# Layer 2's bias: from two TensorE products to a VectorE addition out of PSUM

## The reference, cut to what matters

```
W   = adj * adj                            # nodes x nodes
out = einsum('bnf,nm->bmf', x, W) + bias   # bias: 512 values, one for each feature
x   = layernorm(x + out, axis=-1)          # (x - mean) / sqrt(var + 1e-5)
```

## Time and profile before

| | us |
|---|---|
| median of three runs | 2135.47 |
| the profiled execution, its own time | 2135.43 |
| its span in the trace | 2133.6 |
| TensorE products, busy | 2043.6 (96%) |
| VectorE, busy | 1609.4 (75%) |
| ScalarE, busy | 1061.7 (50%) |
| GpSimd, busy | 131.9 (6%) |

### The profile page before, as it was taken

One profiled execution on the slowest core, in us unless ns is written; L12 is line 12 of the kernel. 1 busy time (PEld: TensorE's weight loads), 2 busy tenths in 40 slices (PEclk: granted clock), 3 DMA queues, 4 the chain that ended last, 5 costly groups with the idle time before them and its releaser, 6 DMA issues.

```text
span 2133.6 us, 34670 instructions
## 1 busy us (share of the span) xinstructions
PE 2043.6 (96%) x13500; PEld 1840.6 (86%) x13500; DVE 1609.4 (75%) x4339; ACT 1061.7 (50%) x1965; POOL 131.9 (6%) x198
## 2 busy tenths in 40 slices
PE   7899999999999999999999999999999999999997
PEld 6788888988888888888988888898888888888896
DVE  6477868778687787878777786877868787787875
ACT  5445536455453645546454553645545364453643
POOL 0000000000000000000100000000000000000000
PEclk9999999999999999999999999999999999999998
DMA  4100000000000000000000000000000000000000
GB/s 139 50 11 11 21 21 11 21 21 21 11 21 21 11 21 11 21 20 11 31 11 20 11 21 21 11 21 21 21 11 21 21 11 20 11 21 20 11 11 20
DMA packets 23652, 44.70 MB, mean 21 GB/s; under 512 B 2624, under 2 KB 2880, under 8 KB 23488
## 3 DMA queue, kind: packets, MB, share of 16 engines
q1 hardware_dynamic: 23488, 42.48, 5.7%
HBM read 25.70 MB, written 16.78 MB: 20 GB/s over the span
## 4 chain that ended last, share of the span: by engine, by line
PE 90%; ACT 4%; DVE 4%; issue 2%; DMA 0%; SPq 0%; POOL 0%; POOLq 0%; ACTq 0%; DVEq 0%
PE psum L494 11%; PE psum L479 11%; PE psum L332 10%; PE psum L419 6%; PE psum L340 6%; PE psum L468 6%; PE psum L519 5%; PE psum L525 5%; PE psum L520 5%; PE psum L469 5%; PE psum L336 5%; PE psum L423 3%; PE psum L506 3%; PE psum L575 2%; ACT xs L693 1%
## 5 line engine op out<-in xcount | busy, mean ns | idle before, releaser
L966 DVE TENSOR_TENSOR zs<-psum,zs 128x512 fp32r<-128x512 f32 (+1 forms) x456 | 262.9, 609 | 191.9 <-ACT zs L693 191.8
L693 ACT ACTIVATE zs<-psum 128x512 fp32r<-128x512 f32 (+1 forms) x456 | 235.8, 535 | 196.7 <-PE psum L479 164.5
L494 PE MATMUL psum<-xs,zs 128*128 128x256 f32 x2048 | 270.8, 285 | 0.0
L494 PEld LDWEIGHTS psum<-xs,zs 128*128 128x128 f32 x2048 | 258.1, 191 | 5.0
L693 ACT ACTIVATE full<-psum 128x512 f32<-128x512 f32 x160 | 94.8, 593 | 284.1 <-PE psum L494 146.5
L340 PE MATMUL psum<-ident,full 128*128 128x128 f32 x1220 | 172.3, 274 | 11.8 <-DMA full<-in_L_gnn_wk_dram 5.1
L419 PE MATMUL psum<-vs,zs 128*128 128x512 f32 x512 | 141.2, 397 | 26.0 <-ACT vs L693 26.0
L340 PEld LDWEIGHTS psum<-ident,full 128*128 128x128 f32 x1220 | 140.0, 141 | 28.5 <-issue 8.2
L693 ACT ACTIVATE vs<-psum 128x512 fp32r<-128x512 f32 x128 | 76.6, 598 | 131.7 <-PE psum L525 131.7
L332 PE MATMUL psum<-vs,zs 128*128 128x512 f32 x512 | 140.2, 396 | 0.7 <-ACT zs L693 0.7
L419 PEld LDWEIGHTS psum<-vs,zs 128*128 128x128 f32 x512 | 91.7, 188 | 54.2 <-DVE full L1225 36.1
(11 more groups left out here) (198 smaller groups left out, 5153.6 us busy)
## 6 DMA issues: line engine op xcount, KB each, us to landing
full<-in_x_dram SPq DMA_DIRECT2D x32, 512.0 KB, 3.5
out_dram<-full SPq DMA_DIRECT2D x32, 512.0 KB, 2.7
full<-in_L_gnn_W_lang_dram SPq DMA_DIRECT2D x2, 1024.0 KB, 5.4
full<-in_L_gnn_W_grav_dram SPq DMA_DIRECT2D x2, 1024.0 KB, 8.1
full<-in_L_gnn_W_O_dram SPq DMA_DIRECT2D x2, 1024.0 KB, 5.4
full<-in_L_gnn_W_V_dram SPq DMA_DIRECT2D x2, 1024.0 KB, 5.0
full<-in_adj_dram SPq DMA_DIRECT2D x1, 256.0 KB, 2.6
full<-in_L_gnn_bias_dram SPq DMA_DIRECT2D x1, 256.0 KB, 6.9
```

The source lines that it names most:

```text
L494: last = mm(halves(bank)[:, n, :], y[:, e, n * P:(n + 1) * P], HTH[s][:, e, :], start=(y is ZH[s][kind] and e == 0 and n == 0), stop=(y is ...
L693: return nc.scalar.activation(dst, src, func, **kw)
L966: return tt(dst, src, plain(hi), ALU.subtract)
```

## The change

The two bias products go, and the first of the other products now opens its bank. The bias stays in SBUF as fp32, spread over all partitions, in a buffer of its own. Before each statistics instruction VectorE adds the bias to the bank and writes the sum into `CUR[r]`; the statistics instruction waits for that sum by a new semaphore, `bias_ready`, and reads `CUR[r]`. Both normalisations read `CUR[r]` and write it in place. The preparation of the bias rows, the setting of `ones_mm` to one and VectorE's wait for the small loads go.

```diff
@@ buffers
-        bias2_mm = sbuf("bias2_mm", [P, U], F32R)
+        bias2_row = sbuf("bias2_row", [P, U])
@@ layer2 (TensorE)
-                for m in range(NT):
-                    mm(psum[s][:, 2 + m, :], ones_mm[0:2, :], bias2_mm[0:2, :], start=True, stop=False)
                 for n in range(NT):
                     pe.wait_ge(x2h_ready[s], j * 2 + (n + 1))
                     for m in range(NT):
                         cols = slice(m * P, (m + 1) * P)
-                        mm(psum[s][:, 2 + m, :], w2_hi[:, n, cols], XH[s][:, n, :], start=False, stop=False)
+                        mm(psum[s][:, 2 + m, :], w2_hi[:, n, cols], XH[s][:, n, :], start=(n == 0), stop=False)
@@ normalise (ScalarE)
-                    src = psum[s][:, 2 + n, :] if layer == 2 else (CUR if layer else X)[s][:, n, :]
+                    src = (CUR if layer else X)[s][:, n, :]
@@ start and prepare_adj (VectorE)
-            nc.vector.memset(plain(ones_mm), 1.0)
-                dve.wait_ge(small_loaded, 16 * 7)
-                link(nc.vector.tensor_copy(bias2_mm[:], bias2_row))
-                link(low(bias2_row, bias2_row, bias2_mm[:]))
-                link(ts(bias2_mm[:], plain(bias2_mm[:]), ident[:, 0:1], None, ALU.mult))
-                link(stt(bias2_mm[:], bias2_row, ident[:, 1:2], plain(bias2_mm[:]), ALU.mult, ALU.add))
@@ norm_stats (VectorE)
                         dve.wait_ge(l2_done[s], j * 2 + (n + 1))
-                        src = psum[s][:, 2 + n, :]
+                        tt(CUR[s][:, n, :], psum[s][:, 2 + n, :], bias2_row[:], ALU.add).then_inc(bias_ready[s], 1)
+                        dve.wait_ge(bias_ready[s], j * 2 + (n + 1))
+                        src = CUR[s][:, n, :]
@@ normalise (VectorE)
-                src = psum[s][:, 2, :] if layer == 2 else X[s][:, 0, :]
+                src = (CUR if layer else X)[s][:, 0, :]
```

More of the change, by code:

```diff
@@ L209, in gnn_stack @@
         x2l_ready = sems("x2l_ready")
+        bias_ready = sems("bias_ready")
         l2_done = sems("l2_done")
@@ L255, in gnn_stack @@
             hi_of["o", l], lo_of["o", l] = ZS[1][:, 0:4, :], ZS[1][:, 4:8, :]
-        bias2_row = full[0][:, 7, :]
-        ones_mm = w_lo[0]["l"][:, 2, P:2 * P]
         DIAG_SLOT = ((3, 1), (1, 0), (2, 0), (3, 0))
@@ L289, in _ @@
                              bm[c * P:(c + 1) * P].unsqueeze(1)).then_inc(small_loaded, 16)
-            sp.dma_start(bias2_row, bias2.unsqueeze(0).to_broadcast([P, U])).then_inc(small_loaded, 16)
+            sp.dma_start(bias2_row[:], bias2.unsqueeze(0).to_broadcast([P, U])).then_inc(small_loaded, 16)
             for l, (g, sg) in enumerate(((gate1, sigma1), (gate3, sigma3))):
```

## The result

The changed kernel takes 2144.72 us (median of five runs, 2143.06 to 2145.78), the kernel before 2134.03 us in the runs beside it: 10.7 us slower, ratio 1.0048 with a 95% interval of 1.0033 to 1.0063. The forecast was 10.2 us more.

The account below looks back on a forecast made before the run. TensorE's product stream, busy 96%, was taken as the bound, with VectorE's chain just in time. Per slot -0.85 + 1.17 = +0.32 us, times 32 = +10.2 us on 2135.43, giving 2145.6 us; 8-in-10 range 2138 to 2153.

Parts of the forecast that it names:

- The bound: Middle slots: TensorE's products run without waits; VectorE's chain behind layer 2 arrives just in time, slack 0 to 0.04 us.
- The products' 0.85 us: Layer 2 on TensorE: removing the two bias products shortens the stream by 0.85 us in each of 32 slots.
- The split into 0.46 and 0.39 us: Within the 0.85 us: 0.46 us for two products in the stream, the rest for entering and leaving the 2-row shape.
- The additions' 0.72 us each: VectorE's chain after layer 2: each bias addition takes 0.686 us plus a 0.034 us gap before its statistics.
- The normalisation's 0.265 us: VectorE's normalisation behind layer 2: reading SBUF instead of PSUM cuts 0.805 to 0.540 us, 0.265 us less.
- Nothing given back in the seams: Seam slots: waits for VectorE and ScalarE stay at 27.6 and 26.0 us, so middle-slot losses are not recovered.
- The size of the hole: Before the middle slots' transposes: TensorE stands 1.17 us, the chain's 1.18 us growth less the slack.
- One sign: Expected in the trace after: transposes wait for VectorE's normalisation 32 times about 1.15 us, some 37 us in total.
- The fifth transpose: It needs ScalarE's half of the normalisation, ending 0.39 us behind VectorE's: just in time, at most 0.04 us late.
- The 2108 us of the hidden chain: Rival: TensorE is the bound and VectorE's longer chain hides, gaining 0.85 us in 32 slots; 2108 us, chance 0.06.
- Free waits: Rival: VectorE's waits on its own writes cost nothing, so +0.09 us a slot; 2138.5 us, chance 0.12.
- A smaller saving: Rival: normalisation saves nothing (2154 us) or only 0.66 us of product time goes (2151.7 us); chance 0.12 for both.

Follow-up runs that it names:

- the products alone: First follow-up: kernel before with its two bias products taken out and no addition, so the bias is left out; 2108.16 us against 2134.05.
- the additions alone: Second follow-up: kernel before with bias products kept and the two additions, their waits and the SBUF reads put in; 2171.30 us, ratio 1.0175.
- the fourth experiment: Changed kernel with eight products that do not depend on layer 2 moved ahead of the transposes in the middle slots; 2106.82 us, ratio 0.9874.
- third experiment: Changed kernel with both additions ahead of both statistics instructions; 2137.15 us against 2134.05 for the kernel before.

## Why the prediction was right

- *The bound.* TensorE's stream without waits in the middle slots, VectorE's chain just in time behind layer 2: shown from both sides, by the products alone (no hole) and the additions alone (only a hole).
- *The products' 0.85 us.* Taken from two like passages of one slot in place of the products' count; run alone it gave 25.9 of the expected 27.3 us, which that run's interval (23 to 29 us) holds, and the passage is 0.67 us in every trace without them. The split into 0.46 and 0.39 us was an argument in the prediction and is now measured.
- *The additions' 0.72 us each.* L1124 gave the length and L1053 the gap. The trace after has 0.683 us for L1032, and 0.72 us from start to start:

```profile
L1032 DVE TENSOR_TENSOR full<-psum,bias_row 128x512 f32<-128x512 f32 x64 | 43.7, 683 | 45.7 <-PE psum L579 45.7
...
L1057 DVE TENSOR_SCALAR full<-full,mv,rstd 128x512 f32<-128x512 f32 x64 | 34.6, 540 | 0.0
```

- *The normalisation's 0.265 us.* The second row has all 64 cases after out of SBUF, at 0.540 us; the saving is gone again with PSUM as source.
- *Nothing given back in the seams.* Their waits are 27.6 and 26.0 us before and after.
- *The size of the hole.* The chain grew by 1.44 - 0.265 = 1.18 us and the hole is 1.16, so the slack was about 0.02 us, inside the 0 to 0.04 that were taken. One sign came out by another count: the profile's waits at the transposes are 32.0 us in total, not some 37, since they run from the modelled end. The 37 us are in the timeline, as 32 times 1.16.
- *The fifth transpose.* ScalarE's end was put just in time, and so it is:

```profile
922.39 0.81 ACT L690 ACTIVATE full<-full,shift,rstd 128x512 f32<-128x512 f32 x1 [6.22 <-DVE shift L1052]
```

It ends at 923.20, 0.38 us behind the normalisation of VectorE, and in all 32 slots the fifth transpose follows the fourth by 0.109 us, as the others follow one another: it does not wait. From the first transpose to the product behind the eighth it is 0.85 us after (922.87 to 923.72) and 0.83 before, medians of the 32 slots for both. These 0.02 us, which the forecast lacks, lie between the first and the second transpose: 0.165 us after and 0.144 before, and 0.108 in the fourth experiment, where no transpose has to wait.
- *The rivals.* The 2108 us of the hidden chain came true in another kernel, the one whose hole was filled (2106.8 us): its mechanism was sound. The prediction had it hang on the length of an addition alone; that the order of TensorE's list decides as well, it did not see. Free waits are out by the second and third experiment. A smaller saving is out by the first and the one with the sum in PSUM.

What stays open is small: the profiled executions differ by 1 to 2 us at the start and the end of the span, outside the slots, and the interval of the result is 7 to 13 us more. So the sum of 10.2 us cannot be told from 10.7.

## What to carry to other kernels

Work that is taken off the busiest engine counts only so far as what replaces it does not lengthen the chain that this engine waits for next. Look in the waits of the weight loads for chains that arrive just in time: here they showed 0.24 us, 32 times, while no product waited. When such a chain must grow, first look for independent work in the same list that can stand ahead of the wait; here one moved line was worth 38 us, and nothing at all without the hole. A small product in an odd shape is priced by the passage around it, not by its columns.

## What the runs showed of the hardware that was not expected

Two products over 128 rows, 126 of them zeros, take 0.39 us less of the stream than the same two over 2 rows, and 32 rows save nothing against 2. In layer 2's chain a VectorE instruction that waits for the one right ahead of it starts some 0.03 us behind its end, and without such a wait 0.08 us before; one instruction in between makes the wait free.
